# Linear attention with a butterfly FFN on one Trainium2 core: up coefficients loaded first, query work in pairs of 1024 columns, keys kept as max(z, -b) on VectorE

## Chip, cores and metric

The kernel runs on one core of one Trainium2 chip. The metric is the time of one execution on the device in microseconds (us); lower is better.

## What is computed

For x of shape (4, 1024, 128), in fp32:

```python
q, k, v = split(x @ W_qkv)                 # 16 heads of 64
q = relu(q @ W_f + b_f);  k = relu(k @ W_f + b_f)
kv = einsum('bhnd,bhne->bhde', k, v)       # no softmax
out = einsum('bhnd,bhde->bhne', q, kv) / (q . k.sum(over n) + 1e-6)
x = layernorm(x + out @ W_out + b_out)
h = butterfly(x @ W_exp + b_exp, up_weights)      # 9 stages over 512
h = butterfly(gelu(h + up_bias), down_weights)
x = layernorm(x + h @ W_con + b_con + down_bias)
```

A butterfly stage multiplies pairs of columns by 2x2 matrices. It is linear, so the kernel applies both butterflies to the weights once: 9 up steps on W_exp (and on b_exp), 9 down steps on W_con. W_f is folded into the query and key weights in the same way, and W_v with W_out into `vo`.

## The kernel before

All engines run their own program, in order, and meet at semaphores. The main part is a loop over 48 slots (`for s in range(SLOTS)`) that every compute engine runs with its own share of each slot; the time of a slot differs from engine to engine. The tokens come in 32 tiles of 128; a batch has 8 tiles, and two chunks of 512 tokens.

- **Keys** (`project_k`, tile kt, two halves of 512 columns): three matmuls of a split product (high and low parts in fp32r) and a fourth, the rank one term `ones_r` by `bf_rows` (L535), that adds the bias b_f. The result lies in one of three PSUM banks, the ring. ScalarE takes it with `k_relu` (L758) into `k`. Slots 0 to 3 have two tiles each, slots 4 to 27 one (tile s + 4).
- **Sum over keys**: VectorE adds tile after tile into `k_total` (`k_sum`, L965 and L969, 128x1024), one slot behind the projection; `ksum` and `ksum_mask` turn it into columns. TensorE adds k^T x into `kx_ps` (`add_kx`, L555, two fp32 matmuls of 512 columns, a tile later than the projection); ScalarE copies it once a batch (`kx_copy`, L778, slots 5, 13, 21, 29), and `head_maps` makes the maps.
- **Queries** (`project_q`, steps i, 16 a batch, two steps in each of slots 4 to 35): split product, then `q_relu` on ScalarE (L765) into a ring of 16 rows `q`.
- **Normaliser** (`norm`, every fourth slot from 8): ScalarE adds eps, VectorE takes the reciprocal (L981), and SyncE's `spread(n)` stores it in four DMAs to DRAM (L395) and loads it back, spread over the partitions, in four of 512 KB (L404) into `recips`.
- **Query times reciprocal** (steps a, two in each of slots 10 to 41): VectorE's `normalise_q(a)` (L995) writes `qn`, ScalarE's `qn_hi` the high part, VectorE's `qn_lo` (L901) the low part. One slot later TensorE's `add_attn(a)` adds the product with the maps. In a slot VectorE does both normalise_q, later qn_lo of the first step, then a residual and its layer norm where there is one, with qn_lo of the second step between the statistics and `layer_norm_end`.
- **Layer norms**: `add_x` in slots 15, 19, ... 43, `residual` in slots 22, 26, ... 42, 44 and 47. VectorE takes the statistics; GpSimd makes `var_eps` (L459) and `rstd` (L462); `layer_norm_end` (L1013) follows on VectorE.
- **FFN**: up_tile, gelu, down, transpose_y from slot 17 on.
- **Butterflies**: GpSimd runs nine `up_step(n)` one after another (two products L451 and a sum L455, each 128x512). VectorE runs `down_step(n)` in slot 1 + n (`DOWN_STEP_SLOT`, two products L914 and a sum L918), at the end of its slot; bias row steps (L930, L934) in slots 2 to 5, and `bias_end` in slot 7. Each step needs 512 KB of coefficients; there are two buffers for each side, so load n waits for the products of step n - 2: `load_up(n)` for `s_up >= 3n - 4`, `load_down(n)` for `s_dn >= 3n - 4` (step m reaches 3m + 2 with its products and 3m + 3 with its sum).
- **SyncE's queue**, in order: the weights and x of batch 0, up 0, down 0, x of batch 1, down 1, up 1, small bias loads, then for n = 2 to 8 down n and up n (after n = 4 the x of batches 2 and 3), and only then `spread(0)`, which waits for the first reciprocal, and the further spreads and stores of the output.

The order of PSUM banks and of the desk bank (a bank for transposes, maps and sums) is written out by hand in the dictionaries `ring_of` and `desk_of`, and `take_ring` waits for the bank's former user by `s_taken`.

Of the kernel before, what the change touches and what calls it, by code (L numbers as in the profile page):

```python
# [5 lines left out]
def postln_linear_attention_butterfly_ffn_kernel(  # L6
# [36 lines left out]
    CH = 512  # L43
# [68 lines left out]
    DOWN_STEP_SLOT = {1 + n: n for n in range(STAGES)}  # L112
# [7 lines left out]
    for s in range(SLOTS):  # L120
# [11 lines left out]
        for use in order:  # L132
            ring_of[use] = len(ring_of)

# [27 lines left out]
    with ctx:  # L162
# [24 lines left out]
        bf_h = sb("bf_h", [128, D], fp32r)  # L187
        bf_rows = sb("bf_rows", [128, CH], fp32r)
        ones_r = sb("ones_r", [128, 128], fp32r)
# [87 lines left out]
        s_bfz = sem("bf_rows_zeroed")  # L277
        s_bfh = sem("bf_hi")
        s_bfl = sem("bf_lo")
# [12 lines left out]
        s_taken = sem("ring_bank_taken")  # L292
        s_dmade = sem("desk_made")
# [38 lines left out]
        def _(sp):  # L332
# [51 lines left out]
            for n in range(2, STAGES):  # L384
                load_down(n)
                load_up(n)
                if n == 4:
                    for b in range(2, BATCH):
                        sp.dma_start(xs[b][:, :, :], xs_view[b, :, :, :]).then_inc(s_xs[b], 16)

            def spread(n):
# [7 lines left out]
                for half in range(2):  # L399
                    g = 2 * n + half  # L400
                    if g >= 2:
                        sp.wait_ge(s_qn, RC * (g - 1))
# [18 lines left out]
        def _(pool):  # L421
# [6 lines left out]
            g.memset(ones_r[:, :].bitcast(fp32), 1.0)  # L428
            g.memset(bf_rows[:, :].bitcast(fp32), 0.0).then_inc(s_bfz, 1)
# [48 lines left out]
        def _(pe):  # L478
# [20 lines left out]
            def take_ring(use):  # L499
                if ring_of[use] >= 3:  # L500
                    pe.wait_ge(s_taken, ring_of[use] - 2)
# [20 lines left out]
            def project_k(kt, half):  # L522
# [11 lines left out]
                split(dst, (xT_h[:, b % 2, tok], xT_l[:, b % 2, tok]), (wk_h[:, cols], wk_l[:, cols]), stop=False)  # L534
                t_.matmul(dst, ones_r[:, :], bf_rows[:, :], start=False, stop=True).then_inc(s_made, 1)  # L535
# [8 lines left out]
            def add_kx(kt):  # L544
# [8 lines left out]
                pe.wait_ge(s_taken, ring_of["k", kt, 1] + 1)  # L553
# [14 lines left out]
            def norm(n):  # L568
                take_ring(("norm", n))
                pe.wait_ge(s_dtaken, desk_of["ksum", n // CHUNKS] + 1)  # L570
                pe.wait_ge(s_taken, ring_of["q", PAIRS * n + PAIRS - 1] + 1)
# [22 lines left out]
            def add_attn(a):  # L594
# [5 lines left out]
                pe.wait_ge(s_qnh, a + 1)  # L600
                pe.wait_ge(s_qnl, a + 1)
# [18 lines left out]
            def transpose_y(n):  # L620
                take_desk(("y", n))
                pe.wait_ge(s_taken, ring_of["down", n] + 1)
# [14 lines left out]
            def down(n):  # L637
# [3 lines left out]
                for i in range(HT):  # L641
                    pe.wait_ge(s_taken, ring_of["up", HT * n + i] + 1)
# [29 lines left out]
            pe.wait_ge(s_bfl, 1)  # L672
# [70 lines left out]
        def _(act):  # L743
# [9 lines left out]
            def k_relu(kt, half):  # L753
                act.wait_ge(s_made, ring_of["k", kt, half] + 1)
                if half == 0 and kt >= KRING:
                    act.wait_ge(s_kxt, 2 * (kt - KRING) + 2)
                    k_summed(act, (kt - KRING) // TILES, (kt - KRING) % TILES)
                a_.activation(k[kt % KRING][:, half * CH:(half + 1) * CH], bank(("k", kt, half))[:, :],  # L758
                              ACT.Relu).then_inc(s_taken, 1)

            def q_relu(i):
                act.wait_ge(s_made, ring_of["q", i] + 1)
                if i >= QRING:
                    act.wait_ge(s_qn, i - QRING + 1)
# [9 lines left out]
            def kx_copy(b):  # L774
                act.wait_ge(s_kxt, 2 * TILES * (b + 1))
                if b:
# [370 lines left out]
```

## Time and profile before

| | us |
|---|---|
| median of 3 runs | 380.69 |
| lowest and highest | 380.1, 384.87 |
| the profiled execution | 380.9 |
| its span, first to last instruction | 379.0 |

| engine | busy us (share of the span) |
|---|---|
| TensorE (PE) matmuls | 333.4 (88%) |
| VectorE (DVE) | 246.2 (65%) |
| ScalarE (ACT) | 173.0 (46%) |
| GpSimd (POOL) | 80.6 (21%) |

Rows below are from the profiled execution, in us from the start of its span. L914 is line 914 of the kernel before; a helper's line stands for all who call it (L483 a split product, L492 transposes, L751 a high part, L901 a low part). SPq is SyncE's queue. A table of stretches gives, after the length of the stretch, the busy time of PE, PEld (weight loads), DVE, ACT and POOL. Matmuls overlap, so the distance of two starts is their true price. In a row "x2" two like instructions are merged, and the duration runs from the first start to the last end. An instruction that follows another on VectorE starts a little before that one is recorded as ended.

### The profile page before, as it was taken

How to read it: one execution, taken by the hardware profiler on the slowest of the kernel's cores; microseconds unless marked ns; L12 is line 12 of the kernel's file. 1: busy time of each engine (PE TensorE's matmuls, PEld its weight loads, DVE VectorE, ACT ScalarE, POOL GpSimd, SP SyncE). 2: the span in 40 equal slices, each digit the busy share in tenths (PEclk: the TensorE clock that was granted, in tenths of full speed). 3: DMA queues.
4: the chain of work that ended last, by engine and by line, in shares of the span. 5: the costliest groups of instructions: out<-in, count | busy, mean ns of one | idle time of the engine just before them, and what ended most of it. 6: DMA issues, size and time to landing. Idle time of an engine off the chain costs nothing.

```text
span 379.0 us, 5158 instructions
## 1 busy us (share of the span) xinstructions
PE 333.4 (88%) x1841; PEld 235.3 (62%) x1841; DVE 246.2 (65%) x489; ACT 173.0 (46%) x289; POOL 80.6 (21%) x77
## 2 busy tenths in 40 slices
PE   4898999299799999999999999999979788589481
PEld 3765677176567767777767675776856565356250
DVE  3536999999956384666518774685585783882613
ACT  2531344034455564674645464646546543434120
POOL 3080565896300002001001100110110110111201
PEclk9999999879989999999999999999999989659766
DMA  5940509333902800630450046006505607500000
GB/s 176 302 143 32 191 17 315 113 112 117 214 9 48 179 0 2 149 78 2 112 115 0 2 110 144 2 3 139 113 2 123 132 3 164 116 0 0 29 28 28
DMA packets 25089, 33.73 MB, mean 89 GB/s; under 512 B 3656, under 2 KB 13928, under 8 KB 25064
## 3 DMA queue, kind: packets, MB, share of 16 engines
q1 hardware_dynamic: 24904, 33.38, 34.6%
q8 instruction: 14, 0.23, 0.2%
q14 instruction: 11, 0.09, 0.1%
q10 hardware_dynamic: 160, 0.03, 0.0%
HBM read 31.04 MB, written 2.36 MB: 88 GB/s over the span
## 4 chain that ended last, share of the span: by engine, by line
PE 52%; DVE 28%; issue 7%; DMA 6%; POOL 4%; ACT 2%; SPq 1%; POOLq 0%; DVEq 0%
PE ring L483 18%; PE kx_ps L555 9%; PE attn_ps L483 8%; DVE late L914 6%; PE ring L643 5%; DMA recips<-recip_rows 4%; DVE qn L995 3%; POOL rstd L462 3%; DVE stats L1004 3%; PE ring L535 2%; PE ring L575 2%; DVE bias_row_term L930 2%; PE desk L492 2%; DVE k_total L969 2%; DVE y_dn L918 2%
## 5 line engine op out<-in xcount | busy, mean ns | idle before, releaser
L765 ACT ACTIVATE q<-ring,bf_col 128x512 f32<-128x512 f32 x64 | 43.9, 686 | 52.3 <-PE ring L483 51.9
L555 PE MATMUL kx_ps<-k,xs 128*128 128x512 f32 x128 | 60.2, 593 | 0.8 <-ACT k L758 0.8
L751 ACT ACTIVATE qn_h<-qn 128x512 fp32r<-128x512 f32 x64 | 39.8, 627 | 36.7 <-DVE qn L995 36.7
L758 ACT ACTIVATE k<-ring 128x512 f32<-128x512 f32 x64 | 38.3, 598 | 34.2 <-PE ring L535 33.8
L901 DVE TENSOR_TENSOR qn_l<-qn,qn_h 128x512 fp32r<-128x512 f32 x64 | 42.9, 680 | 15.8 <-ACT qn_h L751 15.0
L459 POOL TENSOR_TENSOR var_eps<-mean_var,ln_eps 128x4 f32<-128x4 f32 x16 | 7.1, 443 | 205.0 <-DVE mean_var L1008 205.0
L995 DVE TENSOR_TENSOR qn<-q,recips 128x512 f32<-128x512 f32 x64 | 41.1, 684 | 10.5 <-DMA recips<-recip_rows 10.5
L451 POOL TENSOR_TENSOR y<-hid,y_up 128x512 f32<-128x512 f32 x18 | 38.3, 2150 | 39.8 <-DMA hid<-in_L_ffn_up_weights_dram 39.7
L555 PEld LDWEIGHTS kx_ps<-k,xs 128*128 128x128 f32 x128 | 24.1, 189 | 19.2 <-issue 16.5
L483 PE MATMUL ring<-xT_h,wq_h 128*128 128x512 f32 x64 | 35.9, 561 | 0.0
L483 PE MATMUL attn_ps<-qn_h,m_h 128*128 128x512 f32 x64 | 29.2, 456 | 7.6 <-DVE qn_l L901 3.9
L969 DVE TENSOR_TENSOR k_total<-k_total,k 128x1024 f32<-128x1024 f32 x24 | 32.3, 1347 | 0.8 <-ACT k L758 0.6
L483 PE MATMUL ring<-wk_h,xT_h 128*128 128x512 f32 x64 | 29.7, 464 | 3.0 <-ACT q L765 2.0
L643 PE MATMUL ring<-hid,wdn 128*128 128x512 f32 x64 | 30.3, 618 | 0.0
L483 PE MATMUL attn_ps<-qn_l,m_h 128*128 128x512 f32 x64 | 26.7, 417 | 0.0
L483 PE MATMUL attn_ps<-qn_h,m_l 128*128 128x512 f32 x64 | 26.6, 416 | 0.0
L817 ACT ACTIVATE hid<-ring,bup_col 128x512 f32<-128x512 f32 x32 | 22.0, 686 | 9.0 <-PE ring L483 8.8
L483 PE MATMUL ring<-wk_l,xT_h 128*128 128x512 f32 x64 | 25.8, 403 | 0.0
L483 PE MATMUL ring<-wk_h,xT_l 128*128 128x512 f32 x64 | 25.8, 403 | 0.0
L535 PE MATMUL ring<-bf_rows,ones_r 128*128 128x512 f32 x64 | 25.6, 400 | 0.0
L483 PE MATMUL ring<-xT_h,wq_l 128*128 128x512 f32 x64 | 25.5, 399 | 0.0
L483 PE MATMUL ring<-xT_l,wq_h 128*128 128x512 f32 x64 | 25.4, 396 | 0.0
(125 smaller groups left out, 549.7 us busy)
## 6 DMA issues: line engine op xcount, KB each, us to landing
recips<-recip_rows SPq DMA_DIRECT2D x32, 512.0 KB, 7.3
hid<-in_L_ffn_up_weights_dram SPq DMA_DIRECT2D x9, 512.0 KB, 5.3
x<-_L_ffn_down_weights_dram SPq DMA_DIRECT2D x9, 512.0 KB, 4.1
xs<-in_L_attn_x_dram SPq DMA_DIRECT2D x4, 512.0 KB, 7.4
out_dram<-y SPq DMA_DIRECT2D x8, 256.0 KB, 6.1
q<-in_L_attn_W_qkv_dram SPq DMA_DIRECT2D x2, 512.0 KB, 7.9
q<-in_L_attn_W_qkv_dram SPq DMA_DIRECT2D x2, 256.0 KB, 3.3
q<-in_L_attn_W_out_dram SPq DMA_DIRECT2D x2, 256.0 KB, 8.8
```

Of the source, the lines that this page charges most:

```text
L451: g.tensor_tensor(term_up[f].rearrange("p (hi j lo) -> p hi j lo", j=2, lo=lo), w[:, :, :, :, f], yv[:, :, f:f + 1, :].to_broadcast([128, ...
L483: last = t_.matmul(dst, lhsT, rhs, start=start and n == 0, stop=stop and n == len(pairs) - 1)
L535: t_.matmul(dst, ones_r[:, :], bf_rows[:, :], start=False, stop=True).then_inc(s_made, 1)
L555: t_.matmul(kx_ps[half], xs[b % XBUF][:, t, :], k[kt % KRING][:, half * CH:(half + 1) * CH], start=t == 0, stop=t == TILES - 1).then_inc(s ...
L643: last = t_.matmul(bank(("down", n))[:, :], wdn[:, i, :], hid[:, i, :], start=i == 0, stop=i == HT - 1)
L751: a_.activation(dst, src, ACT.Copy).then_inc(done, 1)
L758: a_.activation(k[kt % KRING][:, half * CH:(half + 1) * CH], bank(("k", kt, half))[:, :], ACT.Relu).then_inc(s_taken, 1)
L765: a_.activation(q[:, i % QRING, :], bank(("q", i))[:, :], ACT.Relu, bias=bf_col[:, :])\
L901: v.tensor_tensor(dst, src, high.bitcast(fp32), ALU.subtract).then_inc(done, 1)
L914: v.tensor_tensor(term_dn[j].rearrange("p (hi f lo) -> p hi f lo", f=2, lo=lo), w[:, :, j, :, :], yv[:, :, j:j + 1, :].to_broadcast([128, ...
L969: v.tensor_tensor(k_total[:, :], k_total[:, :], k[kt % KRING][:, :], ALU.add).then_inc(s_ks, 1)
L995: v.tensor_tensor(qn[:, a % 2, :], q[:, a % QRING, :], recips[:, a // RC % 2, a % RC, :], ALU.mult).then_inc(s_qn, 1)
```

## The change

- **Loads.** SyncE's order becomes: up 0, up 1, x of batch 1, the coefficients of the bias, up 2, down 0, bias columns, up 3, down 1, x of batches 2 and 3, then up 4 to up 8, with down 2 behind up 6, down 3 behind up 7 and down 4 behind up 8, then down 5 to down 8, then `spread(0)`. The waits of each load stay as they are. `down_step(n)` moves from slot 1 + n to slot 3 + n.
- **Pairs.** `normalise_q`, `qn_hi` and `qn_lo` work on both steps of a slot at once, as one 128x1024 instruction each; their semaphores count pairs.
- **Keys.** relu(z + b) = max(z, -b) + b. The rank one matmul with the bias goes, and with it `bf_rows`, `bf_h` and `ones_r`. VectorE takes the bank with a maximum against `bf_minus` (-b_f in every partition); ScalarE's `k_relu` is gone. The missing + b is put back in the sums: `kx_end` on VectorE replaces `kx_copy` and adds b times the sum of x over the batch's tokens, which `x_half_sum` takes from the transposed x; `ksum_mask` adds N times b.
- The count of taken banks is split in two semaphores, `s_ktaken` for keys (VectorE) and `s_taken` for the others.

```diff
-    DOWN_STEP_SLOT = {1 + n: n for n in range(STAGES)}
+    DOWN_STEP_SLOT = {3 + n: n for n in range(STAGES)}
...
             load_up(0)
-            load_down(0)
+            load_up(1)
             sp.dma_start(xs[1][:, :, :], xs_view[1, :, :, :]).then_inc(s_xs[1], 16)
-            load_down(1)
-            load_up(1)
...
+            load_up(2)
+            load_down(0)
...
-            for n in range(2, STAGES):
+            load_up(3)
+            load_down(1)
+            for b in range(2, BATCH):
+                sp.dma_start(xs[b][:, :, :], xs_view[b, :, :, :]).then_inc(s_xs[b], 16)
+
+            for n in range(4, STAGES):
+                load_up(n)
+                if n >= 6:
+                    load_down(n - 4)
+            for n in range(STAGES - 4, STAGES):
                 load_down(n)
-                load_up(n)
-                if n == 4:
-                    for b in range(2, BATCH):
-                        sp.dma_start(xs[b][:, :, :], xs_view[b, :, :, :]).then_inc(s_xs[b], 16)
...
-                split(dst, (xT_h[:, b % 2, tok], xT_l[:, b % 2, tok]), (wk_h[:, cols], wk_l[:, cols]), stop=False)
-                t_.matmul(dst, ones_r[:, :], bf_rows[:, :], start=False, stop=True).then_inc(s_made, 1)
+                split(dst, (xT_h[:, b % 2, tok], xT_l[:, b % 2, tok]), (wk_h[:, cols], wk_l[:, cols]))\
+                    .then_inc(s_made, 1)
...
             def qn_hi(a):
-                act.wait_ge(s_qn, a + 1)
+                act.wait_ge(s_qn, a // 2 + 1)
                 if a >= NRING:
-                    act.wait_ge(s_at, a - NRING + 1)
-                hi(qn_h[:, a % NRING, :], qn[:, a % 2, :], s_qnh)
+                    act.wait_ge(s_at, a - NRING + 2)
+                hi(qn_h[:, a % NRING:a % NRING + 2, :], qn[:, :, :], s_qnh)
...
+            def k_max(kt, half):
+                dve.wait_ge(s_made, ring_of["k", kt, half] + 1)
+                if half == 0 and kt >= KRING:
+                    dve.wait_ge(s_kxt, 2 * (kt - KRING) + 2)
+                    k_summed(dve, (kt - KRING) // TILES, (kt - KRING) % TILES)
+                v.tensor_tensor(k[kt % KRING][:, half * CH:(half + 1) * CH].rearrange("p (h d) -> p h d", d=D),
+                                bank(("k", kt, half))[:, :].rearrange("p (h d) -> p h d", d=D),
+                                bf_minus[:, :].rearrange("p (o d) -> p o d", o=1).to_broadcast([128, CH // D, D]),
+                                ALU.max).then_inc(s_ktaken, 1)
+
+            def kx_end(b):
+                dve.wait_ge(s_xpart, CHUNKS * (b + 1))
+                v.tensor_tensor(x_sum[:, b:b + 1], x_part[:, b, 0:1], x_part[:, b, 1:2], ALU.add).then_inc(s_xsum, 1)
+                dve.wait_ge(s_kxt, 2 * TILES * (b + 1))
+                if b:
+                    dve.wait_ge(s_dmade, desk_of["maps", b - 1, 1] + 1)
+                dve.wait_ge(s_xsum, b + 1)
+                v.scalar_tensor_tensor(kx[:, :].rearrange("p (h d) -> p h d", d=D),
+                                       bf_row[:, :].rearrange("p (o d) -> p o d", o=1).to_broadcast([128, HD // D, D]),
+                                       x_sum[:, b:b + 1], kx_both[:, :].rearrange("p (h d) -> p h d", d=D),
+                                       ALU.mult, ALU.add).then_inc(s_kxc, 1)
+
+            def x_half_sum(b, c, src):
+                v.reduce_sum(x_part[:, b, c:c + 1], src, axis=mybir.AxisListType.X).then_inc(s_xpart, 1)
...
-                if a >= 2:
-                    dve.wait_ge(s_qnh, a - 1)
-                    dve.wait_ge(s_qnl, a - 1)
-                v.tensor_tensor(qn[:, a % 2, :], q[:, a % QRING, :], recips[:, a // RC % 2, a % RC, :],
-                                ALU.mult).then_inc(s_qn, 1)
+                if a:
+                    dve.wait_ge(s_qnh, a // 2)
+                    dve.wait_ge(s_qnl, a // 2)
+                v.tensor_tensor(qn[:, :, :], q[:, a % QRING:a % QRING + 2, :],
+                                recips[:, a // RC % 2, a % RC:a % RC + 2, :], ALU.mult).then_inc(s_qn, 1)
```

VectorE's order within a slot becomes: mask, `kx_end`, `k_max` of the first half, `normalise_q` of the pair, reciprocal, x and x1 low parts (with `x_half_sum`), `k_sum`, `qn_lo` of the pair, `k_max` of the second half (and of a second tile in slots 0 to 3), then `add_x` or `residual` with its layer norm, the map's low part, and the down and bias steps last.

## Rows read from the trace of the kernel before

**Rows 1.** Three stretches: busy us of each engine (instructions), granted clock, DMA share, GB/s

```profile
34.00:102.00 68.00, 60.48 (x295) 41.76 (x293) 66.98 (x74) 24.83 (x40) 43.52 (x21) 0.95 0.48 147
102.00:269.00 167.00, 164.84 (x1005) 118.30 (x1006) 101.14 (x205) 93.52 (x157) 10.27 (x13) 0.99 0.32 70
269.00:338.00 69.00, 56.09 (x348) 40.07 (x348) 49.52 (x136) 32.90 (x57) 9.36 (x12) 0.88 0.35 78
```

**Rows 2.** Timeline of TensorE: start us, us, instruction [idle before]

```profile
74.67 1.11 PE L492 MATMUL desk<-ident,xs 128*128 128x128 f32 x4 [7.02 <-DVE ksum_cols L975]
...
76.86 0.63 PE L535 MATMUL ring<-bf_rows,ones_r 128*128 128x512 f32 x1
...
92.12 0.39 PE L535 MATMUL ring<-bf_rows,ones_r 128*128 128x512 f32 x1
```

**Rows 3.** Chain that ended last, tail: start us, us, what

```profile
284.75 0.31 SPq L395
...
288.10 6.70 DMA recips<-recip_rows
294.82 0.71 DVE qn L995
295.55 0.64 ACT qn_h L751
...
296.83 0.69 DVE y L1029
...
298.91 0.56 POOL var_eps L459
```

**Rows 4.** Timelines of GpSimd and VectorE, alone and together

```profile
21.39 1.29 POOL L455 TENSOR_TENSOR y_up<-y 128x512 f32<-128x512 f32 x1
...
79.55 0.68 DVE L901 TENSOR_TENSOR xT_l<-desk,xT_h 128x512 fp32r<-128x512 f32 x1
80.15 1.96 DVE L969 TENSOR_TENSOR k_total<-k_total,k 128x1024 f32<-128x1024 f32 x1
...
81.11 2.15 POOL L455 TENSOR_TENSOR y_up<-y 128x512 f32<-128x512 f32 x1
```

**Rows 5.** Timeline of VectorE: first and last down step, first qn

```profile
33.70 2.07 DVE L914 TENSOR_TENSOR late<-x,y_dn 128x512 f32<-128x512 f32 x2
35.80 0.69 DVE L918 TENSOR_TENSOR y_dn<-late 128x512 f32<-128x512 f32 x1
...
99.64 1.28 DVE L914 TENSOR_TENSOR late<-x,y_dn 128x512 f32<-128x512 f32 x2
...
101.57 1.28 DVE L995 TENSOR_TENSOR qn<-q,recips 128x512 f32<-128x512 f32 x2
102.77 1.22 DVE L969 TENSOR_TENSOR k_total<-k_total,k 128x1024 f32<-128x1024 f32 x1
103.91 1.31 DVE L901 TENSOR_TENSOR qn_l<-qn,qn_h 128x512 fp32r<-128x512 f32 x2
```

**Rows 6.** Groups of instructions, VectorE, butterflies: busy us, mean ns, idle before

```profile
L914 DVE TENSOR_TENSOR late<-x,y_dn 128x512 f32<-128x512 f32 x18 | 21.2, 1217 | 0.1
...
L918 DVE TENSOR_TENSOR y_dn<-late 128x512 f32<-128x512 f32 x9 | 12.1, 1349 | 0.3
...
L930 DVE TENSOR_TENSOR bias_row_term<-coef_rows,bias_rows 4x128 f32<-4x128 f32 x14 | 9.2, 695 | 0.1
...
L934 DVE TENSOR_TENSOR bias_rows<-bias_row_term 4x128 f32<-4x128 f32 x7 | 6.0, 858 | 0.2
```

**Rows 7.** Group of the kx copy on ScalarE

```profile
L778 ACT ACTIVATE kx<-kx_ps 128x1024 f32<-128x1024 f32 x4 | 4.1, 1024 | 0.0
```

**Rows 8.** Timeline of SyncE's queue: last down load, first spread

```profile
86.45 0.33 SPq L367 DMA_DIRECT2D x<-_L_ffn_down_weights_dram  x1
...
91.10 1.73 SPq L395 DMA_DIRECT2D recip_rows<-recip  x4
```

**Rows 9.** Chain that ended last, in the middle

```profile
143.47 0.70 PE ring L483 x3
```

More of the change, by code:

```diff
@@ L133, in postln_linear_attention_butterfly_ffn_kernel @@
             ring_of[use] = len(ring_of)
+    k_taken, taken = {}, {}
+    for use in ring_of:
+        if use[0] == "k":
+            k_taken[use] = len(k_taken) + 1
+        else:
+            taken[use] = len(taken) + 1
+    ring_use = {n: use for use, n in ring_of.items()}
     desk_of = {("wq",): 0, ("v", 0): 1, ("v", 1): 2, ("wcon",): 3}
@@ L500, in take_ring @@
                 if ring_of[use] >= 3:
-                    pe.wait_ge(s_taken, ring_of[use] - 2)
+                    before = ring_use[ring_of[use] - 3]
+                    if before in k_taken:
+                        pe.wait_ge(s_ktaken, k_taken[before])
+                    else:
+                        pe.wait_ge(s_taken, taken[before])
             def transpose_weights(grp, dst):
@@ L621, in transpose_y @@
                 take_desk(("y", n))
-                pe.wait_ge(s_taken, ring_of["down", n] + 1)
+                pe.wait_ge(s_taken, taken["down", n])
                 transpose_tiles(desk, lambda i: yT[:, i * 128:(i + 1) * 128]).then_inc(s_dmade, 1)
@@ L751, in hi @@
                 a_.activation(dst, src, ACT.Copy).then_inc(done, 1)
[L753 to L759, printed above, removed]
             def q_relu(i):
@@ L864, in _ @@
                         attn_copy(n)
-                for kt in k_tiles(s)[1:]:
-                    k_relu(kt, 0)
-                    k_relu(kt, 1)
                 for i in q_steps(s)[1:]:
@@ L991, in normalise_q @@
                     dve.wait_ge(s_rc[a // RC % 2], 32 * (a // RC // 2 + 1))
[L992 to L996 removed]
+                if a:
[3 more added lines that the diff above has]
+                                recips[:, a // RC % 2, a % RC:a % RC + 2, :], ALU.mult).then_inc(s_qn, 1)
             def qn_lo(a):
[L999 to L1000 removed]
+                dve.wait_ge(s_qnh, a // 2 + 1)
+                pair = slice(a % NRING, a % NRING + 2)
+                lo(qn_l[:, pair, :], qn[:, :, :], qn_h[:, pair, :], s_qnl)
             def layer_norm(i, n, src):
@@ L1065, in _ @@
                     ksum_mask(KSUM_SLOT[s])
+                if s in KX_SLOT:
+                    kx_end(KX_SLOT[s])
+                for kt in k_tiles(s)[:1]:
+                    k_max(kt, 0)
                 if s == 0:
@@ L1070, in _ @@
                         lo(wq_l[:, cols], fold[:, :], wq_h[:, cols], s_wl)
-                for a in spreads(s):
+                for a in spreads(s)[:1]:
                     normalise_q(a)
@@ L1078, in _ @@
                     x1T_lo(X1T_SLOT[s - 1])
-                for kt in kx_tiles(s):
+                for kt in kx_tiles(s)[:1]:
                     if kt % TILES:
@@ L1083, in _ @@
                     qn_lo(a)
+                for kt in k_tiles(s)[:1]:
+                    k_max(kt, 1)
+                for kt in k_tiles(s)[1:]:
+                    k_max(kt, 0)
+                    k_max(kt, 1)
+                for kt in kx_tiles(s)[1:]:
+                    if kt % TILES:
+                        k_sum(kt)
                 if s in ATT_T_SLOT:
@@ L1087, in _ @@
                     residual(YT_SLOT[s])
-                for a in spreads(s)[1:]:
-                    qn_lo(a)
                 if s in ATT_T_SLOT:
```

74 lines of the change are left out of this document (28 added, 46 removed).

## Prediction

> **What bounds the kernel now.** I read the table of stretches first, then the groups of the slowest stretch, then the timelines of VectorE, GpSimd and SyncE there, and last the chain of waits in the tail. The stretches [rows 1] show three regimes. From 34 to 102 us VectorE is busy 66.98 of 68 us: VectorE sets the pace, and TensorE, though busy, waits for it now and then (one gap of 7.02 us, with matmuls at 1.2 GHz behind it: 0.63 us each where others take 0.4 [rows 2]). From 102 to 269 us TensorE is busy 164.84 of 167 us and VectorE 101.14. From 269 us on nothing is full; the end is set by a chain through VectorE, ScalarE, GpSimd and a DMA [rows 3].
>
> The first regime is full because of GpSimd. Its product of the up butterfly and VectorE's sums take turns: at 80.15 a k_total sum takes 1.96 us where the same instruction takes 1.22 at 102.77 [rows 4, 5]; it ends a little after GpSimd's pair of products, and the GpSimd sum at 81.11 in turn takes 2.15 us where one alone takes 1.29 (at 21.39) [rows 4]. The xT_l subtraction at 79.55, which reads PSUM and one SBUF tile, takes 0.68 us beside the same GpSimd products. So VectorE pays a wait for GpSimd on instructions with two SBUF operands, and none on one that reads PSUM. The y_dn sum shows it as a mean: 1349 ns over nine [rows 6], 0.69 us for the first, with GpSimd idle [rows 5].
> The Trainium skill says this as a rule ("SBUF — State Buffer", "Who interferes with whom"): a VectorE instruction with two SBUF inputs and a GpSimd instruction that reads SBUF hold a shared port pair exclusively, and one with at most one SBUF input does not contend. By that rule the new maximum (PSUM and one SBUF operand) is free of GpSimd; if it were not, 20 of them in this stretch, half of them meeting GpSimd for some 0.8 us, would add 8 us. The xT_l row sides with the rule.
>
> **A. Up to the first attention step (slots 2 to 9 of VectorE).** Clean prices from start to start: 0.60 us for 128x512 (two qn in 1.20, 101.57 to 102.77), 1.14 us for 128x1024 (102.77 to 103.91); a down step 2.7 us (products 33.70 to 35.80, sum 0.6 to the next start) [rows 5]; a bias step I take at 0.9 us, three small instructions (an estimate: with GpSimd waits its three cost 2.2 us on average, 15.2 us over seven [rows 6]).
> Before: 9 k_total sums 10.3, eight down steps at 2.7 and the last at 1.9 (99.64 to 101.57) 23.5, bias steps 6.3, the rest (two copies, two xT_l and one m_l at 0.60, mask, reciprocal, bias end) some 5.2: 45.3 us. It took 101.6 - 33.7 = 67.9 us. The other 22.6 us are waits for GpSimd, of at most 27 (21 GpSimd instructions of 1.29 us [rows 1, 4]).
> After: k_total 10.3; only down steps 0 to 6 (each is two slots later) 18.9; bias 6.3; rest 5.2; 20 maxima (tiles 4 to 13) at 0.60, 12.0; two x sums 1.2; kx_end 1.2: 55.1 us. The maximum is not in the trace; it is bounded by 0.60 (the pitch of a plain 128x512 instruction) and 0.69 (its full duration) and I take 0.60; kx_end by 1.02 (the ScalarE copy it replaces [rows 7]) and 1.38 (two halves). GpSimd: step 2 now runs before slot 2, since its coefficients come first, so 18 instructions, 23 us, are left; VectorE's 14 us of PSUM work lie beside them in part. I take 15 us of wait, bounds 5 (GpSimd almost done when the down steps come) and 23. GpSimd does not come through at once: SyncE issues load_up(7) behind load_down(2), which waits for down step 0 in slot 3, and load_up(8) behind load_down(3).
> VectorE starts slot 2 at 33.2 (the transposes of slot 1 set this; the bf rows and rank one terms before it were beside them) and ends slot 9 at 33.2 + 55.1 + 15 = 103.3, against 101.6: +1.7 us, bounds -8 and +10.
>
> **B. The wait that is new.** SyncE works in order. spread(0), which stores the reciprocals and reads them back spread over the partitions, stands behind all coefficient loads. The last, load_down(8), waits for s_dn >= 20, the products of down step 6. Before, step 6 was in slot 7, and SyncE issued that load at 86.45 and was free when the reciprocal of slot 8 came, for a first store at 91.10 [rows 8]. Now step 6 stands at the end of slot 9, and the first instruction of slot 10 but one, normalise_q(0), needs the result. From the first store to the first qn the path takes 294.82 - 284.75 = 10.07 us, of which the spreading transfer is 6.70 [rows 3]. So qn starts 10.1 us after the products, plus 0.35 for issuing the load; of this the sum of step 6 hides 0.7, so 9.7 us after slot 9's end. Nothing else covers it: one maximum stands between. Queued behind normalise_q on VectorE are k_total, qn_lo and the second maximum, so the attention steps, and after three ring banks the projections, stand too. Bounds 8 and 13 (the 512 KB of load_down(8) lie ahead in the same queue). From first qn to first attention step it takes about 3.6 us against 4.0, -0.4.
> First attention step: +1.7 + 9.7 - 0.4 = **+11.0 us**. TensorE will have idled over 10 us and comes back at 1.2 GHz; the gap of 7.02 us cost 11 matmuls 0.2 us each [rows 2], so **+2** (0 to 3).
>
> **C. The middle.** The rank one term is one matmul of 0.233 us (0.70 for three [rows 9]) per half tile. TensorE is the bound for tiles 16 to 31, 32 halves: **-7.5 us**. The 32 before lie where VectorE or the new wait is late. ScalarE is rid of its 64 k copies; it was busy 24.83 of 68 and 93.52 of 167 us [rows 1], so that is worth nothing. VectorE gains them: it had 66 us free of 167 and gets some 26 (34 maxima 20, x sums 2, kx_end 4), so on average TensorE stays the bound. But slots 22/23 and 26/27 each hold two layer norms in a row and down steps 7 and 8 now fall in slots 10 and 11: I take **+1.5**, bounds 0 and 9.
>
> **D. The tail, pairs.** Where VectorE's chain is the bound (slots 30, 31, 34, 35, 38, 39), a slot runs: qn of step a (0.73 to the hand-over), qn_h 0.64, qn_l, then the residual: 296.83 - 294.82 = 2.01 us [rows 3]. The second half's qn_h and qn_l lay beside these and under GpSimd's rstd. As a pair: qn 1.26, qn_h about 1.10 (a 128x1024 copy is 1.02 [rows 7]), qn_l 1.14 to the next start: 3.5 us, **+1.5**. Back come 0.35: GpSimd's var_eps takes 0.56 [rows 3] beside the qn_l of the second half and should take some 0.2 without it (an estimate, four elements per partition). So +1.1 in six slots, 6.6, and +1.2 at the last attention steps: **+7.8 us**, bounds 2 (if ScalarE's half hides after all) and 11.
> Pairs elsewhere save 0.06 us per pair (1.14 for 1.20): nothing.
>
> Sum against the profiled execution (380.9 us, 379.0 of it span; the median of the three runs is 380.69): 380.9 + 11.0 + 2 - 7.5 + 1.5 + 7.8 = 395.7, so **396 us**. A measurement of this kernel tells about 2% from no change: 373 to 388.
>
> **Rivals.**
> 1. *GpSimd gets out of the way (not slower).* With the up coefficients first, GpSimd might be done by slot 4; then its waits are 5 us instead of 15 and slot 9 ends at 93. The wait of B still comes but from an earlier point: first attention step +1. Then 380.9 + 1 + 1 - 7.5 + 1.5 + 7.8 = 385, and with the low bound in D 379. For it: 22.6 us of VectorE's first regime are such waits. Against: SyncE's order holds up steps 7 and 8 back behind down loads, and the down steps' products are strided and slow on their own (2.07 with GpSimd idle). It decides if waits fall under about 8 us.
> 2. *VectorE takes over the middle.* If every double layer norm stalls the ring, the 7.5 us are lost and the upper bound of C comes: 380.9 + 13 - 7.5 + 9 + 7.8 = 403, with waits at their upper bound in A 410. For it: three ring banks and in-order maxima; against: VectorE was idle 66 us there.
> 3. *The pairs cost nothing in the tail.* If the chain there shifts to another engine, D is 2 instead of 7.8: 390. For it: TensorE has 13 of 69 us idle there [rows 1]; against: the chain names VectorE, ScalarE and GpSimd in every slot.
> That the change does not do what it says I leave out: the terms of b add up.
>
> **Chances.** Forecast 0.55 (388 to 404); rival 1 0.20 (376 to 388, mostly within 2%); rival 2 0.13; rival 3 0.12 (386 to 392). Slower by over 2%: 0.55 + 0.13 + half of rival 3 and a little of rival 1, 0.77; within 2%: 0.18; faster: 0.05. Range 382 to 407: from the upper half of rival 1 to the lower half of rival 2.
>
> **What the new profile would show.** Right: VectorE idle 8 to 13 us before the first qn, put down to the DMA recips, behind a load of down coefficients issued in slot 9; the recip stores far later than the first reciprocal; TensorE's gap in the same place; from there to 269 us of before TensorE full again and shorter by some 6 us; layer-norm slots of 7.9 us in place of 6.8 at the end. Wrong: the first qn at or before 103 us (B or A fails); VectorE over 95% busy in the middle (C); tail slots of 6.8 us (D).

## Result and the profile after

| | before | after |
|---|---|---|
| median of 4 runs, us | 381.08 | 414.52 |
| lowest and highest | 380.1, 384.87 | 412.43, 416.52 |
| the profiled execution | 380.9 | 414.27 |
| its span | 379.0 | 412.5 |
| first qn (VectorE, slot 10) | 101.57 | 119.14 |
| first qn to the qn of slot 30 | 167.4 | 173.6 |
| qn of slot 30 to the end | 110.0 | 119.7 |

The ratio is 1.086 [1.077, 1.095]: slower, and 18.5 us beyond the forecast of 396.0. The last three rows cut the span at the same instructions in both kernels. They differ by +17.6, +6.2 and +9.7 us, which is the whole 33.5 us.

The stretches of the kernel after, cut at these points (the columns of [rows 1]: PE, PEld, DVE, ACT, POOL, granted clock, DMA share, GB/s):

```profile
34.00:107.40 73.40, 57.94 (x260) 36.94 (x258) 64.21 (x89) 12.10 (x19) 32.93 (x19) 0.88 0.24 84
107.40:119.10 11.70, 2.11 (x10) 1.44 (x10) 0.64 (x2) 0.00 (x0) 0.00 (x0) 0.74 0.71 169
119.10:292.80 173.70, 159.00 (x969) 112.16 (x970) 129.99 (x217) 68.77 (x98) 8.49 (x13) 0.97 0.30 66
292.80:371.00 78.20, 57.59 (x347) 41.49 (x345) 48.49 (x114) 31.88 (x46) 7.23 (x12) 0.86 0.33 72
371.00:412.00 41.00, 26.80 (x80) 16.41 (x80) 15.61 (x60) 9.90 (x14) 4.83 (x8) 0.75 0.07 20
```

The reader is to see three things against [rows 1]. In the first stretch VectorE is busy 64.21 of 73.4 us, no longer all of the time. Then follow 11.7 us in which nearly nothing runs, with the clock at 0.74. In the middle TensorE is busy 159.00 us of 173.7: less work than the 164.84 of before, but 14.7 us idle where there had been 2.2. Of these, 3.8 us lie before its first attention step at 122.86.

Groups of VectorE in the first stretch (busy us, mean ns | idle before):

```profile
L903 DVE TENSOR_TENSOR late<-x,y_dn 128x512 f32<-128x512 f32 x14 | 18.0, 1328 | 0.0
L955 DVE TENSOR_TENSOR k<-ring,bf_minus 128x512 f32<-128x512 f32 x19 | 12.7, 679 | 0.7 <-PE ring L496 0.7
L919 DVE TENSOR_TENSOR bias_row_term<-coef_rows,bias_rows 4x128 f32<-4x128 f32 x14 | 9.2, 690 | 0.1
...
L1132 DVE COPY vo<-spare_ps 128x512 f32<-128x512 f32 x1 | 0.7, 692 | 3.1 <-PE spare_ps L535 3.1
L1135 DVE COPY vo<-spare_ps 128x512 f32<-128x512 f32 x1 | 0.7, 692 | 2.6 <-PE spare_ps L535 2.6
```

The maximum takes 679 ns here beside GpSimd, and 683 ns over all 64. The two copies into `vo` waited 3.1 and 2.6 us for TensorE; before, no group of VectorE waited there.

Timeline of SyncE's queue, and of GpSimd (in brackets the idle time before and what ended it):

```profile
77.18 29.89 SPq L377 DMA_DIRECT2D x<-_L_ffn_down_weights_dram  x5
107.12 1.81 SPq L410 DMA_DIRECT2D recip_rows<-recip  x4
111.17 2.56 SPq L419 DMA_DIRECT2D recips<-recip_rows  x4
```

```profile
62.73 3.00 POOL L464 TENSOR_TENSOR y<-hid,y_up 128x512 f32<-128x512 f32 x2 [6.04 <-DMA hid<-in_L_ffn_up_weights_dram]
...
74.05 4.46 POOL L464 TENSOR_TENSOR y<-hid,y_up 128x512 f32<-128x512 f32 x2 [6.17 <-DMA hid<-in_L_ffn_up_weights_dram]
```

The five down loads take SyncE from 77.18 to 107.07, most of it the waits for down steps; the first reciprocals, ready at 95.22, are stored at 107.12, against 91.10 in [rows 8]. GpSimd's steps 7 and 8 wait 6.04 and 6.17 us for up coefficients that stand behind down loads.

Timeline of VectorE: the end of slot 9, a slot of the middle, a slot of the tail:

```profile
103.99 0.69 DVE L890 TENSOR_TENSOR m_l<-desk,m_h 128x512 fp32r<-128x512 f32 x1 [2.06 <-ACT m_h L767]
...
106.75 0.69 DVE L907 TENSOR_TENSOR y_dn<-late 128x512 f32<-128x512 f32 x1
107.36 0.68 DVE L955 TENSOR_TENSOR k<-ring,bf_minus 128x512 f32<-128x512 f32 x1
119.14 1.23 DVE L1012 TENSOR_TENSOR qn<-q,recips 128x1024 f32<-128x1024 f32 x1 [11.09 <-DMA recips<-recip_rows]
...
228.47 0.68 DVE L955 TENSOR_TENSOR k<-ring,bf_minus 128x512 f32<-128x512 f32 x1
229.07 1.21 DVE L1012 TENSOR_TENSOR qn<-q,recips 128x1024 f32<-128x1024 f32 x1
230.20 0.68 DVE L973 TENSOR_REDUCE x_part<-desk 128x1 f32<-128x512 f32 x1
230.80 0.68 DVE L890 TENSOR_TENSOR xT_l<-desk,xT_h 128x512 fp32r<-128x512 f32 x1
...
301.10 1.21 DVE L1012 TENSOR_TENSOR qn<-q,recips 128x1024 f32<-128x1024 f32 x1
303.44 1.22 DVE L890 TENSOR_TENSOR qn_l<-qn,qn_h 128x1024 fp32r<-128x1024 f32 x1 [1.12 <-ACT qn_h L767]
304.58 0.68 DVE L1038 TENSOR_TENSOR x<-desk,xs 128x512 f32<-128x512 f32 x1
...
307.98 1.12 DVE L1031 TENSOR_SCALAR x<-x,mean_var,rstd 128x128 f32<-128x128 f32 x4 [1.40 <-POOL rstd L475]
309.01 1.23 DVE L1012 TENSOR_TENSOR qn<-q,recips 128x1024 f32<-128x1024 f32 x1
```

At 119.14 is the wait that was forecast. At 228.47 a slot of the middle begins: maximum, qn of a pair, sum over x, and only then the low part of x (L890), which lets TensorE have the desk bank back. From 301.10 to 309.01 runs a slot of the tail with a layer norm, 7.91 us. In it VectorE waits 1.12 us for ScalarE's high part, then takes 1.14 us for the low part, and only behind these starts `add_x` and its statistics.

Timeline of TensorE at three gaps:

```profile
45.24 0.80 PE L496 MATMUL ring<-wk_h,xT_h 128*128 128x512 f32 x1 [4.09 <-DVE k L955]
...
122.86 0.77 PE L496 MATMUL attn_ps<-qn_h,m_h 128*128 128x512 f32 x1 [12.65 <-DVE qn_l L890]
...
231.54 0.66 PE L505 MATMUL desk<-ident,late 128*128 128x128 f32 x4 [3.67 <-DVE xT_l L890]
```

The last of these is one of three such waits (us in all, times, longest):

```profile
PE desk L505 <- DVE xT_l L890: 7.1, 3, 3.7
```

They stand at 157.03 (1.72 us), 191.06 (1.73) and 231.54 (3.67). The rest of the idle time of the middle is one wait of 1.79 us for a maximum (167.89) and one of 2.04 us for VectorE's `add_x`, which frees the desk bank for the maps (274.04).

### The profile page after: what moved, and what is told of

The parts are those of the page before. It is cut to its first block, busy times and chain, and to the rows that moved or that the text cites. A ratio compares the mean times of both kernels' runs of the same rounds, so it can differ in the third digit from the quotient of the medians.

```text
span 412.5 us, 4883 instructions
## 1 busy us (share of the span) xinstructions
PE 328.9 (80%) x1777; PEld 226.9 (55%) x1777; DVE 280.3 (68%) x504; ACT 129.0 (31%) x189; POOL 70.8 (17%) x75
## 4 chain that ended last, share of the span: by engine, by line
PE 50%; DVE 29%; DMA 6%; issue 6%; POOL 4%; ACT 3%; SPq 1%; POOLq 0%; DVEq 0%; ACTq 0%
PE ring L496 18%; PE kx_ps L572 9%; PE attn_ps L496 7%; PE ring L660 5%; DVE late L903 4%; DMA recips<-recip_rows 3%; DVE k L955 3%; DVE qn L1012 3%; POOL rstd L475 3%; DVE qn_l L890 3%; PE ring L592 2%; DVE stats L1022 2%; ACT qn_h L767 2%; PE desk L606 2%; DVE bias_row_term L919 2%
## 5 line engine op out<-in xcount | busy, mean ns | idle before, releaser
L572 PE MATMUL kx_ps<-k,xs 128*128 128x512 f32 x128 | 64.6, 630 | 8.3 <-issue 5.6
L955 DVE TENSOR_TENSOR k<-ring,bf_minus 128x512 f32<-128x512 f32 x64 | 43.5, 683 | 14.6 <-PE ring L496 14.4
L1012 DVE TENSOR_TENSOR qn<-q,recips 128x1024 f32<-128x1024 f32 x32 | 39.0, 1217 | 20.0 <-DMA recips<-recip_rows 19.7
L890 DVE TENSOR_TENSOR qn_l<-qn,qn_h 128x1024 fp32r<-128x1024 f32 x32 | 39.1, 1222 | 16.2 <-ACT qn_h L767 16.0
L767 ACT ACTIVATE qn_h<-qn 128x1024 fp32r<-128x1024 f32 x32 | 33.7, 1054 | 46.7 <-DVE qn L1012 46.6
L472 POOL TENSOR_TENSOR var_eps<-mean_var,ln_eps 128x4 f32<-128x4 f32 x16 | 3.2, 199 | 223.9 <-DVE mean_var L1026 223.9
L572 PEld LDWEIGHTS kx_ps<-k,xs 128*128 128x128 f32 x128 | 25.3, 201 | 29.4 <-issue 24.8
L464 POOL TENSOR_TENSOR y<-hid,y_up 128x512 f32<-128x512 f32 x18 | 30.7, 1729 | 27.9 <-DMA hid<-in_L_ffn_up_weights_dram 27.1
L496 PEld LDWEIGHTS attn_ps<-qn_h,m_h 128*128 128x128 f32 x64 | 13.0, 204 | 31.1 <-issue 23.6
L985 DVE TENSOR_TENSOR k_total<-k_total,k 128x1024 f32<-128x1024 f32 x24 | 29.4, 1224 | 0.0
```

Source lines behind the costliest of these rows:

```text
L464: g.tensor_tensor(term_up[f].rearrange("p (hi j lo) -> p hi j lo", j=2, lo=lo), w[:, :, :, :, f], yv[:, :, f:f + 1, :].to_broadcast([128, ...
L496: last = t_.matmul(dst, lhsT, rhs, start=start and n == 0, stop=stop and n == len(pairs) - 1)
L572: t_.matmul(kx_ps[half], xs[b % XBUF][:, t, :], k[kt % KRING][:, half * CH:(half + 1) * CH], start=t == 0, stop=t == TILES - 1).then_inc(s ...
L767: a_.activation(dst, src, ACT.Copy).then_inc(done, 1)
L890: v.tensor_tensor(dst, src, high.bitcast(fp32), ALU.subtract).then_inc(done, 1)
L955: v.tensor_tensor(k[kt % KRING][:, half * CH:(half + 1) * CH].rearrange("p (h d) -> p h d", d=D), bank(("k", kt, half))[:, :].rearrange("p ...
```

## The experiments

The theory after the result: (1) the reciprocals stand behind the last down loads; (2) the pair's chain qn, qn_h, qn_l stands ahead of the layer norm; (3) with the keys, TensorE waits in each slot for something that VectorE does later than before. The rivals are costs of the parts themselves: more work on VectorE, or contention from moved transfers. "Fs" below is the first qn, "mid" the time from there to the qn of slot 30, "tail" the rest of the span, all from the profiled execution; before has 101.6, 167.4 and 110.0. Each time stands beside the kernel before on the same chip.

**Loads alone (e1_loads_only).** The Loads part of the diff on the kernel before.

> The kernel before with the new load order and the down steps two slots later, nothing else. Theory 1 (each part has its own price; this one's is SyncE's order): slots 2 to 9 of VectorE lose two down steps (6.6 us) and some waits for GpSimd, so slot 9 ends near 92 us, then VectorE waits about 10 us for the recips before its first qn, at 102 to 104 us; the time is 381 to 386. Rival 1 (GpSimd out of the way is what counts): no wait, or one that costs nothing, time 370 to 375. Rival 2 (all of the loss is VectorE's added load): 381, with no wait of over 3 us for recips.

392.37 us against 379.51, ratio 1.033 [1.028, 1.038]. Slot 9 ends at 101.6, as before; VectorE then waits 10.69 us. SyncE:

```profile
70.83 30.51 SPq L367 DMA_DIRECT2D x<-_L_ffn_down_weights_dram  x5
101.38 1.82 SPq L400 DMA_DIRECT2D recip_rows<-recip  x4
```

The new wait is there (theory 1) and slots 2 to 9 did not get shorter, so that the expected 381 to 386 was too low. VectorE did lose work: from 34 to 102 us it is busy 57.12 us for 66.98. But it now stands idle instead, 4.64 us for `m_h`, 2.25 for the normaliser and 1.77 for a `vo` bank, while TensorE is as busy as before (61.06 us for 60.48), and the chain that ended last runs through TensorE from 76.1 to 97.6. TensorE stood right behind VectorE in this stretch.

**Pairs alone (e2_pairs_only).** The Pairs part on the kernel before.

> The kernel before with qn, its high and its low part in pairs of 1024 columns, nothing else. Theory 1: nothing until 269 us, then each slot with a layer norm takes 7.9 us in place of 6.8, six of them, and the last steps 1 to 3 us more: 388 to 392. Rival 2 (the loss is VectorE's added load): the pairs take load off, so 379 to 382.

391.75 us, 1.033 [1.031, 1.036]. Fs 102.2, mid 167.4, tail 120.5: nearly all of the loss is in the tail, as expected.

**Keys alone (e3_keys_only).** The kernel after without the Loads and Pairs parts.

> The change without its load order and without its pairs: no rank one matmuls, the maximum on VectorE. Theory 1: slots 2 to 9 of VectorE are 12 to 15 us longer, the recips are in time, TensorE saves 7.5 us in the middle and loses about as much in new waits for the desk bank, whose x low part now stands behind a maximum and a sum on VectorE: 391 to 398. Rival 2 (added load everywhere): 405 or more. Rival 3 (the middle keeps its saving): 385 to 390.

400.1 us, 1.051 [1.044, 1.058], a little above what was expected. Fs 117.2, mid 172.2, tail 110.5. No wait for reciprocals: of the 15.7 us ahead of the first qn, 14.4 are the 20 maxima (12 us at 0.60 from start to start), the sums over x and `kx_end` at their clean prices. Stretch of the middle, and two waits of the whole run (us, times, longest):

```profile
117.20:289.40 172.20, 161.43 (x979) 112.80 (x979) 127.73 (x251) 70.28 (x119) 10.28 (x13) 0.98 0.28 62
```

```profile
PE ring L491 <- DVE k L952: 14.1, 6, 4.9
...
PE desk L500 <- DVE xT_l L887: 7.1, 3, 3.6
```

So the rank one terms did leave TensorE (161.43 us of work, 164.84 before), but 10.8 us of idle time came, 7.1 of them three waits for the low part of x. Of the waits for the maximum only one, 1.8 us, lies in the middle; the other 12.3 us stand ahead of the first qn.

**The first reciprocals ahead of the last down load (e4_spread_ahead).** The kernel after with

```diff
-            for n in range(STAGES - 4, STAGES):
+            for n in range(STAGES - 4, STAGES - 1):
                 load_down(n)
...
                     spread(n)
+                if n == 0:
+                    load_down(STAGES - 1)
```

> The changed kernel with the first spread of the reciprocals issued ahead of the last down load. Theory 1: the wait of 11 us before the first qn goes and nothing else takes its place, since VectorE is the engine that is late there: 401 to 405. Rival 4 (the wait covered other work that is now late, such as down steps 7 and 8 or TensorE's backlog): 410 to 415. The last down load comes later then, and down step 8 waits for it by at most a few us.

405.54 us, 1.069 [1.067, 1.071], just above the theory's range, and 9.0 us less than after. The profiled execution, the slowest of the four (407.35), is 6.9 us below that of after: 8.2 less in Fs (110.9 for 119.1), 2.2 more in mid (175.8), 0.9 less in the tail (118.8). 2.94 us of the wait are left, because load_down(7) still stands ahead.

**Keys alone, low part of x first (e5_keys_x_first).** On e3, in VectorE's slot:

```diff
                 if s in KX_SLOT:
                     kx_end(KX_SLOT[s])
+                if s - 1 in XT_SLOT:
+                    xT_lo(*XT_SLOT[s - 1])
                 for kt in k_tiles(s)[:1]:
                     k_max(kt, 0)
...
-                if s - 1 in XT_SLOT:
-                    xT_lo(*XT_SLOT[s - 1])
```

> The run with the keys alone (400.1 us), with the low part of x (and its sum, which must read the desk bank first) moved to the head of VectorE's slot, ahead of the first maximum. Theory 1 (the middle loses to the desk bank, which the transposes of slots 15, 19 and 23 wait for, 7.1 us in all, because the low part stands behind a maximum that waits for TensorE): these waits go, 393 to 395. Rival 5 (VectorE is simply full in the middle): the wait moves to the next instruction, 398 to 401.

391.75 us against 379.38, 1.032 [1.027, 1.037]: 8.3 us less than e3, a little more than the theory gave. Its middle:

```profile
116.20:281.10 164.90, 158.67 (x979) 111.19 (x979) 128.61 (x251) 70.21 (x119) 10.72 (x13) 1.00 0.30 65
```

165 us instead of 172: TensorE's idle time fell from 10.8 to 6.2 us (one wait of 1.8 us for the low part is left of the 7.1), and its own work from 161.43 to 158.67, at a granted clock of 1.00 for 0.98. Two instructions in another order give back more than the keys cost in the middle (167.4 before).

**Keys alone, first maximum late (e6_keys_max_late).** On e3, from slot 4 on `k_max(kt, 0)` stands behind qn, reciprocal, low parts and k_sum.

> The run with the keys alone, from slot 4 on with the first maximum moved behind the qn products, the reciprocal, the low parts of x and x1 and the sum over keys. Theory 1 in its wider form (VectorE can no longer run ahead of TensorE, since the first thing it does in a slot is to wait for that slot's first projection): the desk waits go and the reciprocal is early again, 391 to 395. Rival 5: 398 or more. A new wait of TensorE for the bank of the first half would show as a wait of q behind k; I expect under 2 us of it.

409.59 us, 1.077 [1.071, 1.083], where 391 to 395 was expected: a miss. Mid is 180.6 us. The waits say why (whole run; 14.1 us in 6 in e3):

```profile
PE ring L491 <- DVE k L952: 26.8, 10, 4.9
```

In the middle alone they are 12.3 us in 5, for 1.8 us in 1 in e3. The wider theory, that whatever the maximum delays must be ahead of it, is false. The ring has three banks, and its maximum frees one of them; what had to be earlier was the desk's low part alone.

**Pairs alone, low part late (e7_pairs_low_late).** On e2, in VectorE's slot:

```diff
-                for a in spreads(s)[:1]:
-                    qn_lo(a)
...
                 if s in YT_SLOT:
                     residual(YT_SLOT[s])
+                for a in spreads(s)[:1]:
+                    qn_lo(a)
```

> The run with the pairs alone (391.8 us), with the low part of the pair moved behind the residual's and the first norm's statistics, where VectorE waits for GpSimd's rstd. Theory 1 (the tail pays for ScalarE's high part, 1.1 us, standing bare between two VectorE instructions in each of six slots with a layer norm, and a doubled low part): such a slot takes 6.0 to 6.3 us in place of 7.9, and the time is 378 to 381. Rival 6 (the pairs cost by making TensorE wait for both steps): the late low part makes that worse, 392 or more.

379.49 us, 1.002 [0.998, 1.005]: against the kernel before the pairs cost nothing any more. The slot in the timeline of VectorE, and GpSimd beside it:

```profile
276.23 1.22 DVE L993 TENSOR_TENSOR qn<-q,recips 128x1024 f32<-128x1024 f32 x1
277.37 0.68 DVE L1019 TENSOR_TENSOR x<-desk,xs 128x512 f32<-128x512 f32 x1
...
279.30 1.19 DVE L899 TENSOR_TENSOR qn_l<-qn,qn_h 128x1024 fp32r<-128x1024 f32 x1
281.67 1.12 DVE L1012 TENSOR_SCALAR x<-x,mean_var,rstd 128x128 f32<-128x128 f32 x4 [1.18 <-POOL rstd L462]
282.70 1.22 DVE L993 TENSOR_TENSOR qn<-q,recips 128x1024 f32<-128x1024 f32 x1
```

```profile
279.46 1.09 POOL L459 TENSOR_TENSOR var_eps<-mean_var,ln_eps 128x4 f32<-128x4 f32 x1 [4.29 <-DVE mean_var L1007]
280.62 1.01 POOL L462 TENSOR_TENSOR rstd<-var_eps,minus_half 128x4 f32<-128x4 f32 x1
```

6.47 us from qn to qn. The pair's low part now lies in the time in which VectorE would wait for GpSimd's rstd anyway, and ScalarE's high part lies beside `add_x`.

**Before, both low parts late (e8_low_late).** The same without pairs.

> The kernel before with both low parts of a slot moved behind the statistics, single steps as before. Theory 1: ScalarE's high part and both low parts lie beside GpSimd's work, a slot with a layer norm takes 6.1 us in place of 6.8 in the tail: 375 to 378. Rival 6 (TensorE waits for the low part of the first step): 379.5 to 384.

377.58 us, 0.997 [0.993, 1.000]. Four of the six slots with a layer norm take 6.3 us, the others 6.7 and 6.9. This is the fair partner of e7, with the same late low parts: beside it the pairs still cost 1.9 us, half a per cent, where e2 beside the kernel before cost 12.2. So the order, and not the pairing, was most of their price, and the pairing itself gains nothing.

**Loads alone, the first reciprocals ahead of down loads 7 and 8 (e9_loads_spread_ahead).** On e1:

```diff
-    DOWN_STEP_SLOT = {3 + n: n for n in range(STAGES)}
+    DOWN_STEP_SLOT = {3 + n + (n > 6): n for n in range(STAGES)}
...
-            for n in range(STAGES - 4, STAGES):
+            for n in range(STAGES - 4, STAGES - 2):
                 load_down(n)
...
+                if n == 0:
+                    load_down(STAGES - 2)
+                    load_down(STAGES - 1)
```

> The kernel before with the new load order alone (e1_loads_only), but with spread(0) put ahead of the loads of down coefficients 7 and 8, and down steps 7 and 8 one slot later (slots 11 and 12). If the whole loss of e1 (392.4 against 379.5 us) is the reciprocals queued behind these two loads (a wait of 10.7 us ahead of the first qn), the first qn comes at 101 to 103 us of the span and the time is 379 to 383 us. If the load order costs something of its own behind the first qn (down steps 7 and 8 lie then in the middle, beside attention work, and 512 KB each beside the reciprocals), it is 385 to 390 us with the first qn as early.

378.32 us against 380.11, 0.994 [0.990, 0.998], just below the theory's range. SyncE:

```profile
69.90 13.28 SPq L367 DMA_DIRECT2D x<-_L_ffn_down_weights_dram  x3
88.18 1.73 SPq L400 DMA_DIRECT2D recip_rows<-recip  x4
```

The stretch from 34 to 102 us, with VectorE busy 58.61 us of 68 and TensorE 60.44:

```profile
34.00:102.00 68.00, 60.44 (x292) 41.83 (x291) 58.61 (x69) 25.13 (x41) 33.27 (x18) 0.92 0.38 109
```

Fs 101.1, mid 166.1, tail 110.1. Against e1 (112.4, 168.1, 111.1) that is 11.3 us of the wait itself, and 1.9 and 1.1 behind it. The order of the loads as such costs nothing, and it gains next to nothing either, since TensorE's work fills the time that VectorE was spared; where the reciprocals stand in the queue costs all of it.

**The kernel after with the three mends (e10_all_mended).** After, with the edits of e5, e7 and e9.

> The changed kernel with the three mends together: spread(0) ahead of the loads of down coefficients 7 and 8 (their steps in slots 11 and 12), the low part of x and its sum at the head of VectorE's slot, the pair's low part behind the statistics of the residual or norm. Theory: three causes, whose prices add: 414.5 less 11 (the wait for reciprocals), less 8 (e5 against e3), less 10 (e7 against e2, a little less since the keys' maxima stand there too) is 385.5; 383 to 390 us. What is left over the kernel before is the longer first regime, some 6 us up to slot 9 (the 20 maxima). Rival: VectorE has too much to do in the middle when maxima and pairs meet, and takes back what is won: 395 to 400 us, with waits of TensorE for VectorE between the first qn and slot 30.

385.52 us, 1.015 [1.008, 1.021], as expected (383 to 390). First stretch and middle:

```profile
34.00:107.40 73.40, 58.04 (x262) 37.19 (x260) 64.04 (x90) 12.11 (x19) 31.64 (x18) 0.91 0.35 102
107.40:275.00 167.60, 160.53 (x979) 112.07 (x980) 129.00 (x218) 69.33 (x98) 13.45 (x13) 0.99 0.32 71
```

Mid is 167.5 and tail 108.0. So 29.0 of the 33.4 us are three places in two queues, with one reservation: 2.4 us of the shorter tail lie behind the last qn (39.1 us for 41.5), where the time varies from run to run (last section). What is left lies ahead of the first qn (107.4 for 101.6).

**Keys of tiles 16 to 31 alone, low parts late (e11_keys_half_low_late).** On e8; tiles 0 to 15 keep `k_relu` and the rank one term, and x sums, `kx_end` and N times b come for batches 2 and 3 alone:

```diff
-                t_.matmul(dst, ones_r[:, :], bf_rows[:, :], start=False, stop=True).then_inc(s_made, 1)
+                if kt < MAXED:
+                    t_.matmul(dst, ones_r[:, :], bf_rows[:, :], start=False, stop=True).then_inc(s_made, 1)
```

(`MAXED` is 16.)

> The kernel before with late low parts (e8_low_late, 377.6 us) and the keys of tiles 16 to 31 alone (slots 12 to 27, where TensorE is the bound) as maximum on VectorE without the rank one term, the low part of x at the head of the slot; tiles 0 to 15 stay with ScalarE, so that the first regime keeps its work. Theory: the maxima are costly only where VectorE is the bound (the first regime); in the middle the 32 rank one terms (7.5 us of TensorE) are worth the 2 to 3 us that e5 showed there (164.95 against 167.4), so 373 to 377 us with the first qn at 101 to 103 us. Rival: a bank that has to wait for VectorE's slot order costs the middle as much as the terms gave, whatever the load of VectorE: 379 to 385 us.

374.43 us against 380.11, 0.986 [0.979, 0.992], as expected; the fastest kernel of the study, though by less than the 2% that count as a clear change. First stretch, middle and end:

```profile
34.00:102.00 68.00, 60.67 (x296) 41.78 (x294) 66.97 (x73) 25.00 (x40) 43.10 (x21) 0.95 0.49 145
102.00:267.30 165.30, 158.93 (x974) 111.75 (x975) 125.68 (x246) 72.58 (x123) 12.68 (x13) 0.99 0.32 68
...
333.70:372.30 38.60, 23.36 (x80) 14.21 (x78) 15.71 (x63) 10.49 (x16) 4.82 (x8) 0.83 0.08 21
```

The first stretch is that of before (66.97 of 68 us), and mid is 165.3, 2.1 us under e8. The other 2.6 us by which its tail is under e8's come from slot 37 (9.3 us for 12.0), which no run explains.

**e10 with the keys of tiles 16 to 31 alone (e12_all_mended_keys_half).**

> The mended changed kernel (e10_all_mended, 385.5 us, first qn at 107.4 us, slot 30 167.5 us later) with the maximum on VectorE for tiles 16 to 31 alone; tiles 0 to 15 keep ScalarE's relu and the rank one term. Theory: what e10 still loses to the kernel before is the 20 maxima of the first regime, so the first qn comes at 101 to 102.5 us, the middle takes 165 to 168 us and the time is 376 to 380 us, below e10 by 6 to 9 us. Rival: the remaining loss of e10 is the longer middle, since pairs and maxima meet there; then this kernel gains less than 4 us over e10 (382 to 386 us).

378.62 us against 378.96, 0.997 [0.992, 1.002]: 6.9 us below e10, as expected.

```profile
34.00:100.30 66.30, 58.62 (x290) 40.52 (x288) 58.15 (x67) 25.71 (x41) 33.62 (x18) 0.95 0.39 113
100.30:267.00 166.70, 160.90 (x983) 112.42 (x982) 125.91 (x212) 71.79 (x102) 13.47 (x13) 0.99 0.32 71
```

Fs 100.3 (107.4 in e10), mid 166.7, tail 111.2: what e10 had left over was the price of the maxima in the first stretch. (The profiled execution took 380.31 us, and 42.4 us of its tail lie behind the last qn, where e10 has 39.1.)

## Why the prediction was wrong

The direction was right, and so were the mechanisms of B and D, each a little too small. A had a term too few, and one step, C, had the wrong sign. In us from first qn to first qn and so on:

| | forecast | measured |
|---|---|---|
| A, end of slot 9 | +1.7 | +5.8 |
| B, to the first qn | +9.7 | +11.8 |
| start of attention, clock, C | -4.4 | +6.2 |
| D, tail | +7.8 | +9.7 |

**The step that failed is C**: "ScalarE is rid of its 64 k copies ... VectorE gains them: it had 66 us free of 167 and gets some 26 ..., so on average TensorE stays the bound." It was put at -7.5 for the terms and +1.5 for waits; with the start of attention and the clock that made -4.4, and +6.2 came. The saving was real: 161.43 us of TensorE work in e3, and 158.67 in e5 at full clock, 6.2 less than before, where 7.5 were forecast. But the waits were 12 us and not 1.5: an average of free time says nothing of an order. The engines run in order, and the maximum, the pair's qn and the sum over x stand ahead of the low part of x, which TensorE's desk bank waits for: three waits, 7.1 us, of which the one at 231.54 alone is 3.67. Moving that part to the head of the slot gave back 7.3 us of the middle in e5. I had looked for the delay in the double layer norms of slots 22/23 and 26/27 (+1.5). Two of the three waits are in slots 15 and 19, which have one layer norm; but the longest falls in slot 23, and the 2.04 us at 274.04 in slot 27, so that the long slots before these may have a part in them. No run separates this. (From the first qn on there are 35 maxima, not 34.) Another 3.8 us of TensorE's idle time in the changed kernel run from the first qn to its first attention step; before, it had projections to do in that time and was idle 2.0 us. Rival 2 came nearest in time (403) and named the regime, but its mechanism, layer norms that stall the ring, isn't what the timeline shows: only 1.79 us of the middle are a wait for a ring bank.

**A** was mis-sized by 4.1 us: two terms were too high, by 1.8 and 3.3 us, and one of 9.2 us was missing. VectorE started slot 2 at 31.4, not 33.2. It took 76.0 us to the end of slot 9: 66.8 busy and 9.2 idle. Against 55.1 us of clean work that is 11.7 us above it, put down to waits for GpSimd and below my 15. The 9.2 idle us were not in the sum at all: VectorE and TensorE take turns (TensorE waited 4.09 us for a maximum at 45.24, then VectorE 3.1 and 2.6 us for the `vo` banks, and 2.06 for `m_h`). I had taken VectorE as busy throughout because it was before. The idle time isn't the maxima's doing alone: e1 has none of them, and VectorE waits 4.64, 2.25 and 1.77 us there. Rival 1 falls: in the changed kernel GpSimd was through by 80.2 us, waits shrank, and slot 9 still ended later; in e1 and e9 VectorE was spared 8 to 10 us of work, and TensorE set the end of the stretch. e3 shows the keys' price without the loads' help, 15.7 us.

**B** was right in place, cause and nearly in size: 11.78 us from slot 9's end for 9.7. The path from the first store to the first qn took 12.02 us, where the tail's path in [rows 3], from which I took it, had 10.07; from the first store's issue to the spreading transfer it is 4.68 for 3.35, and the transfer takes 7.31 for 6.70. The +2 for the clock is right in mechanism but not against the kernel before. Behind the gap the granted clock is 0.50 from 122.86 to 126.5, with TensorE busy throughout, which costs some 1.8 us (half of the 3.6). But in the kernel before it is 0.51 from 103.54 to 107.0, behind a gap of 2.04 us, which costs about as much. What is new against before is a later stretch at 0.50, from 232.6 to 235.8, behind the gap of 3.67 us. These costs are estimates from the busy time at 0.50.

**D** was right: slots of 7.91 us for the 7.9 forecast, `var_eps` at 0.20 us. The six slots with a layer norm lose 7.7 us for my 6.6. In slots 30 and 34 VectorE waits 1.54 and 1.63 us for `qn_h` where it waits 1.12 in the others: the Pairs part also puts ScalarE's `qn_hi` behind the first `q_relu` of the slot, which I had left out. The other slots of the tail lose the rest (2.0 for 1.2). Rival 3 is false in the kernel as it stands, but e7 shows that it is the order that makes it so.

That the maximum is free of GpSimd held: 679 ns on average in the first stretch. The rule of the Trainium skill ("SBUF — State Buffer", "Who interferes with whom") agrees with this row.

The parts alone cost 12.9, 12.2 and 20.6 us, together 33.4 and not 45.7. Slot 9 ends at 107.4 with all three and at 117.2 in e3: two down steps leave the first stretch (5.4 us), and GpSimd is through at 80.2 instead of 109.2 us, so that VectorE's sums and products meet it less (a down step's product takes 1328 ns on average for 1599, a `k_total` sum 1210 for 1389). The wait of B then gives it back. The maxima also cost less beside the new loads, 7.1 us of Fs (e10 against e12) for the 15.7 of e3, since they lie in part in the time that VectorE was idle in e9.

## What to carry to other kernels

An instruction that moves to an engine with free time still takes a place in that engine's order: look not at the share of idle time but at what stands behind it, and which bank or transfer the other engines wait for there. A transfer issued in order behind a wait inherits that wait, so short and urgent ones go ahead of loads that have slack. Put work that nobody waits for, such as a low part, into the gap in which its engine waits anyway.

## What was not expected of the hardware

GpSimd's `var_eps`, four elements a partition, takes 0.20 us in the kernel after, 0.56 us before ([rows 3]) where a 128x512 subtraction of SBUF operands starts beside it on VectorE, and 1.09 us in e7 beside a 128x1024 one. In both it ends 0.06 us after the subtraction (299.47 after 299.41, 280.55 after 280.49): a tiny instruction waits until the large one is through. The Trainium skill's rule of the exclusive port pair ("SBUF — State Buffer", "Who interferes with whom") would make it so, here seen from GpSimd's side. In e7 the wait is harmless, because the whole slot is shorter all the same.

The last 80 matmuls of the program took TensorE 26.80 us at a granted clock of 0.75 in the kernel after (from 371 on), but 23.36 us at 0.83 in e11 (from 333.7 on), and the stretch to the end was 3 us shorter there. Over all traces the time from the last qn to the end is 38.4 us (e8, granted clock 0.87) to 42.4 us (e12, 0.74). What came just before doesn't sort them: between slots 30 and 41 the clock was 0.92 in e11 and 0.94 in e12. I made no run to separate it, and the cause stays open; in comparisons of tails up to 4 us may be this. The kernels before and after both take 41.5 us there, so that D is free of it.
